# An attention loop laid out anew: other places for the transposes, the mask and the turned values

## The reference

```python
def _dequant_matmul(x, qw, scales):
    w = (qw.astype(jnp.float32) - ZERO) * jnp.repeat(scales, GS, axis=0)
    return x @ w
q = _dequant_matmul(hidden_states, qw_q, scales_q)   # 32 heads of 128
k = _dequant_matmul(hidden_states, qw_k, scales_k)   # 8 heads
v = _dequant_matmul(hidden_states, qw_v, scales_v)   # 8 heads
...
q, k = _apply_rope(q, cos, sin), _apply_rope(k, cos, sin)
k, v = jnp.repeat(k, rep, axis=1), jnp.repeat(v, rep, axis=1)
scores = jnp.einsum('bhqd,bhkd->bhqk', q, k) / math.sqrt(HD)
scores = jnp.where(causal[None, None], scores, jnp.finfo(scores.dtype).min)
attn = jax.nn.softmax(scores.astype(jnp.float32), axis=-1)
ctx = jnp.einsum('bhqk,bhkd->bhqd', attn, v)
return _dequant_matmul(ctx, qw_o, scales_o)
```

## Time and profile before

| | us |
|---|---|
| median of three executions | 559.31 |
| lowest, highest | 554.47, 561.33 |
| the profiled execution: its own time | 560.78 |
| its span on the core | 558.7 |
| PE busy | 534.9 (96%) |
| DVE, ACT, POOL busy | 477.6, 429.0, 383.3 |

### The profile page before, as it was taken

One profiled execution on the slowest core, in us unless ns is written; L12 is line 12 of the kernel. 1 busy time (PEld: TensorE's weight loads), 2 busy tenths in 40 slices (PEclk: granted clock), 3 DMA queues, 4 the chain that ended last, 5 costly groups with the idle time before them and its releaser, 6 DMA issues.

```text
span 558.7 us, 10860 instructions
## 1 busy us (share of the span) xinstructions
PE 534.9 (96%) x3190; PEld 332.7 (60%) x3190; DVE 477.6 (85%) x629; ACT 429.0 (77%) x1091; POOL 383.3 (69%) x400
## 2 busy tenths in 40 slices
PE   8999979999999999999999999999999999987985
PEld 6744456666666666666666666666666666653442
DVE  4885957999899899989998999899989998876897
ACT  3574558878888888788878887888788878876795
POOL 3005485799779877987799779867986897741063
PEclk9989999999999999999999999999999999999899
DMA  8931344742673267327733672367336532410003
GB/s 295 271 74 38 82 107 133 170 95 57 170 178 88 57 177 175 79 66 177 176 69 75 176 181 61 82 177 168 70 82 169 131 79 72 96 38 1 1 20 132
DMA packets 41341, 63.47 MB, mean 114 GB/s; under 512 B 12452, under 2 KB 20804, under 8 KB 41316
## 3 DMA queue, kind: packets, MB, share of 16 engines
q1 hardware_dynamic: 35652, 46.94, 32.3%
q0 software_dynamic: 3648, 12.75, 11.3%
q10 hardware_dynamic: 2016, 3.48, 2.0%
HBM read 28.55 MB, written 2.10 MB: 55 GB/s over the span
## 4 chain that ended last, share of the span: by engine, by line
PE 82%; DVE 8%; ACT 4%; issue 2%; DMA 2%; POOL 1%; ACTq 0%; SPq 0%; DVEq 0%; POOLq 0%
PE pair L1578 22%; PE pair L1579 22%; PE flow L1702 11%; PE flow L1567 9%; PE flow L1694 6%; PE pair L1485 3%; PE pair L1507 1%; DVE y_max L1361 1%; DMA swap_q<-raw_q 1%; PE flow L1572 1%; DVE accT L1265 1%; ACT probs L779 1%; PE flow L1485 1%; DVE probs L1373 1%; DVE rope_c L1373 1%
## 5 line engine op out<-in xcount | busy, mean ns | idle before, releaser
L1265 DVE SCALAR_TENSOR_TENSOR accT<-pair,so_now,accT 128x1024 f32<-128x1024 f32 x103 | 130.9, 1277 | 19.8 <-PE pair L1579 16.2
L1249 DVE SCALAR_TENSOR_TENSOR raw_q<-pair,sc_now,raw_q 128x1024 f32<-128x1024 f32 x90 | 115.4, 1282 | 7.0 <-ACT raw_q L835 3.9
L572 POOL TENSOR_TENSOR rope_s<-swap_q,consts 128x512 f32<-128x512 f32 x62 | 85.4, 1378 | 30.6 <-DMA swap_q<-raw_q 30.6
L1578 PE MATMUL pair<-ctx_hi,wo 128*128 128x512 f16 x256 | 97.0, 379 | 4.2 <-issue 2.3
L1579 PE MATMUL pair<-ctx_lo,wo 128*128 128x512 f16 x256 | 97.0, 379 | 0.0
L1578 PE MATMUL pair<-h_hi,wq 128*128 128x512 f16 x240 | 91.0, 379 | 0.2 <-ACT raw_q L835 0.2
L779 ACT ACTIVATE probs<-flow,negmax 128x128 f32<-128x128 f32 x248 | 87.3, 368 | 4.9 <-DVE negmax L1217 4.9
L1579 PE MATMUL pair<-h_lo,wq 128*128 128x512 f16 x240 | 91.0, 379 | 0.0
L584 POOL TENSOR_TENSOR qT<-rope_c,rope_s 128x512 f32<-128x512 f32 x62 | 85.5, 1379 | 4.6
L572 POOL TENSOR_TENSOR rope_c<-raw_q,consts 128x512 f32<-128x512 f32 x62 | 77.6, 1274 | 10.7 <-DVE raw_q L1249 10.3
L1702 PEld LDWEIGHTS flow<-probsT,v_now 128*128 128x128 f32 x512 | 62.9, 193 | 19.2 <-ACT probsT L841 15.3
(11 more groups left out here) (281 smaller groups left out, 1008.5 us busy)
## 6 DMA issues: line engine op xcount, KB each, us to landing
swap_q<-raw_q SPq DMA_DIRECT2D x62, 256.0 KB, 3.7
accT<-part_out POOLq DMA_DIRECT2D x22, 512.0 KB, 4.5
wq_i<-in_L_attn_qw_q SPq DMA_DIRECT2D x8, 1024.0 KB, 5.6
wo_i<-in_L_attn_qw_o SPq DMA_DIRECT2D x32, 256.0 KB, 2.8
swap_k<-raw_k SPq DMA_DIRECT2D x14, 256.0 KB, 3.6
wkv_i<-in_L_attn_qw_k SPq DMA_DIRECT2D x8, 256.0 KB, 3.7
wkv_i<-in_L_attn_qw_v SPq DMA_DIRECT2D x8, 256.0 KB, 4.1
stage<-in_x ACTq DMA_DIRECT2D x4, 256.0 KB, 4.7
```

The source lines that it names most:

```text
L572: pool.tensor_tensor(per_seq(into[:, f, :]), per_seq(source[:, f, :]), on_each_seq(table), ALU.mult).then_inc(done, 1)
L1249: dve.scalar_tensor_tensor(out=into, in0=flat(pair[pair_of(h, (kind, j), last, first)][:, :, :]), scalar=sc_now[:, scale_slot(kind, h), j: ...
L1265: dve.scalar_tensor_tensor(out=a, in0=flat(pair[pair_of(h, (O, c), last, first)][:, :, :]), scalar=so_now[:, (h if c == 0 else h - 1) % 2, ...
L1578: pe.matmul(into[:, f, :], w, upper[:, half[f]], start=True, stop=False)
```

## The change

All lists of the loop are written anew.

- TensorE: `turn_probs(0)` stands one step earlier (behind `(Q, 1)`), with two steps between it and `context(0)`; `turn_probs(1)` no longer follows `context(0)` directly but one step later, and `(O, 2)` stands between it and `context(1)`. Heads 2 and 3 of the last group keep their order.
- The mask: ScalarE writes it in head 3 as well (`SEEDED` is gone). The matmul that added it goes, in all groups but the last.
- The values: one step `(VALUES, 0)` of eight transposes into `pair[2]` in head 3, copied by ScalarE as one 128x1024 instruction in place of two of 128x512.
- ScalarE: the exponentials of half 0 come first in a head; `dequant` of the weights moves from the head's start to its end (`output_weights`, `dequant_q`) or between (`dequant_kv`); `part_output` comes after the output weights.
- VectorE: `inverse(1)` comes behind the drain of `(Q, 1)`; `inverse(0)` of the next head is taken at the end of a head, between the drain of `(O, 0)` and `maxima(1)`; `(O, 2)` is added before `split_context(1)`.
- POOL: in head 0 `normalise(0)` comes before the sine product. SP: `load_q` and `load_kv` before the swaps of head 1, `load_output` behind them.

```diff
@@ the steps
-                  [(Q, 0), (O, 1), (Q, 1), (Q, 2), (Q, 3), (V, 0), (V, 1), (O, 2), (O, 3), (V, 2), (O, 0)],
-                  [(Q, 0), (O, 1), (Q, 1), (Q, 2), (V, 3), (Q, 3), (O, 2), (O, 3), (O, 0)]]
+                  [(Q, 0), (O, 1), (Q, 1), (Q, 2), (Q, 3), (V, 0), (O, 2), (V, 1), (O, 3), (V, 2), (O, 0)],
+                  [(Q, 0), (O, 1), (Q, 1), (Q, 2), (V, 3), (Q, 3), (O, 2), (VALUES, 0), (O, 3), (O, 0)]]
...
-            return at % 3 if at < len(STEPS) - 1 else 1
+            return at % 3 if at < len(STEPS) - 1 else 2
...
-        SEEDED = REP - 1
-
         def seeded(h, last):
 
-            return h < SEEDED and not (last and h >= 2)
+            return not (last and h >= 2)
@@ POOL
-                    if first and h == 0:
+                    if h == 0:
                         normalise(0)
                     if ahead:
                         q_sine(0)
-                    if not (first and h == 0):
+                    if h > 0:
                         normalise(0)
@@ ScalarE
-                    def keep_values(turned, f):
-
-                        act.wait_ge(vT_done, 2 * turned + f + 1)
-                        act.activation(v_now[:, HB * f:HB * f + HB, :], per_seq(flow[f][:, :]), ACT.Copy).then_inc(v_kept, 1)
+                    def keep_values():
+
+                        act.wait_ge(step_done, steps_by(g, h, (VALUES, 0), first, last))
+                        act.activation(v_flat, flat(pair[pair_of(h, (VALUES, 0))][:, :, :]), ACT.Copy).then_inc(act_drained, 1)
...
                     if not (first and h == 0):
                         exps(n, 0, score_bank(0, last and h == 3))
-                        if present(h, (Q, 0), first, last):
-                            drain_query()
+                    if h < 2 and not last and not (first and h == 0):
+                        dequant_kv(g + 1, h)
+                    if present(h, (Q, 0), first, last):
+                        drain_query()
                     exps(n, 1, score_bank(1, last and h == 3))
...
+                    seed_mask(0)
                     keep_upper_context(1)
+                    output_weights()
                     if h == 3 and not last:
-                        keep_values(g + 1, 0)
-                    if not (first and h == 0):
-                        seed_mask(0)
+                        keep_values()
+                    part_output()
                     seed_mask(1)
-                    part_output()
+                    if h < REP - 1 and present(h + 1, (Q, 0), False, last) or h == REP - 1 and not last:
+                        dequant_q(g + (h + 3) // REP, (h + 3) % REP)
@@ VectorE
-                    inverse(0)
+                    if first and h == 0:
+                        inverse(n, 0)
                     add_output(1)
-                    if not (first and h == 0):
-                        inverse(1)
...
                         drain(*((V, 3) if h == 3 and j == 3 else (Q, j)))
-                        if first and h == 0 and j == 1:
-                            inverse(1)
+                        if j == 1 and not (last and h >= 2):
+                            inverse(n, 1)
...
                     add_output(0)
+                    if not (last and h == 3):
+                        inverse(n + 1, 0)
                     if not (last and h >= 2):
                         maxima(n + 1, 1)
@@ TensorE
-                            turn_values(f, flow[f])
+                    def values_ahead():
+
+                        pe.wait_ge(dve_drained, drains_by(g, h, (V, 3), first, last))
+                        free_pair(VALUES, 0)
...
+                    project(Q, 1)
+                    if not (first and h == 0):
+                        turn_probs(0)
+                    project(Q, 2)
+                    if first and h == 0:
+                        turn_probs(0)
+                    project(*((V, 3) if h == 3 else (Q, 3)))
+                    context(0)
+                    project(*((K, 0), (K, 2), (V, 0), (Q, 3))[h])
+                    turn_probs(1)
+                    output(2)
                     if h == 2:
-                        project(V, 0)
                         project(V, 1)
+                    context(1)
                     if h == 3:
-                        project(Q, 3)
-                    context(1)
...
+                        values_ahead()
+                    output(3)
                     scores_ahead(0)
```

More of the change, by code:

```diff
@@ L264, in present @@
                 return False
-            return not (last and (s[0] in (K, V) or s[0] == Q and h >= 2))
+            return not (last and (s[0] in (K, V, VALUES) or s[0] == Q and h >= 2))
         def added_by_dma(h, s, last):
@@ L480, in body @@
                     n = REP * g + h
-                    if h < 2 or not last:
-                        load_output(g + h // 2, (h + 2) % REP)
                     if h == 1 and not last:
                         load_q(g + 1)
+                        if loads:
+                            load_kv(g + 2)
                     if present(h, (Q, 3), first, last):
@@ L494, in body @@
                         swap(swap_k, raw_k, swapped_k)
+                    if h < 2 or not last:
+                        load_output(g + h // 2, (h + 2) % REP)
             body(0, True, False)
@@ L1288, in body @@
                         drain(K, 2)
+                    if h == 3:
+                        drain(Q, 3)
+                    if not (last and h >= 2):
+                        add_output(2)
                     if h == 2:
                         drain(V, 1)
-                    if h == 3:
-                        drain(Q, 3)
                     split_context(1)
                     if not (last and h >= 2):
-                        add_output(2)
                         add_output(3)
@@ L1697, in context @@
                     def context(f):
-                        if h == 0:
-                            pe.wait_ge(v_kept, 2 * g + f + 1)
+                        if first and h == 0:
+                            pe.wait_ge(v_kept, f + 1)
+                        elif h == 0:
+                            pe.wait_ge(act_drained, drains_by(g, -1, (VALUES, 0), first, last))
                         pe.wait_ge(probsT_kept, 2 * n + f + 1)
@@ L1704, in context @@
                         mm.then_inc(pv_done, 1)
-                    def values_ahead(f):
-                        if h == 3 and not last:
-                            if f == 0:
-                                pe.wait_ge(dve_drained, drains_by(g, h, (V, 3), first, last))
-                            pe.wait_ge(ctx_split, 2 * n + f + 1)
-                            turn_values(f, flow[f])
+                    def values_ahead():
+                        pe.wait_ge(dve_drained, drains_by(g, h, (V, 3), first, last))
+                        free_pair(VALUES, 0)
+                        into = pair[pair_of(h, (VALUES, 0))]
+                        for f in range(2):
+                            for b in range(HB):
+                                mm = pe.transpose(into[:, f, seq(b)], raw_v[:, f, seq(b)], ident)
+                        mm.then_inc(step_done, 1)
                     def scores_ahead(f):
@@ L1729, in body @@
                     output(1)
-                    project(Q, 1)
-                    project(Q, 2)
-                    if not last:
-                        turn_probs(0)
-                    project(*((V, 3) if h == 3 else (Q, 3)))
                     if last and h >= 2:
@@ L1737, in body @@
                         output(3)
-                    if last:
                         turn_probs(0)
```

73 lines of the change are left out of this document (24 added, 49 removed).

## The result

The changed kernel takes 543.02 us (median of four executions, 541.43 to 544.40). The kernel before, in the same session, takes 558.54 us. The ratio is 0.9736, with a 95% interval of 0.9691 to 0.9780, so the change is faster by 2.6%. The forecast was 546 us, range 543 to 555. The profiled execution took 544.21 us, with a span of 542.4 us.

A forecast was written before the change was run, and what follows sets the result against it. TensorE, without idle time in the loop, was taken to bound the kernel. Savings of 11.0 (groups 1 to 6), 1.5 (group 0), 1.1 (first head) and 0.3 us (last group) make 13.9, giving 546 us, range 543 to 555.

The forecast's parts named there:

- The slots: On TensorE, context of half 0 and transposes of half 1 together save 0.32 us a head, 1.28 a group.
- The masks: Two mask matmuls of 0.28 us, pause included, leave TensorE in each of groups 0 to 6: 0.56 a group.
- Costs at nothing: ScalarE's mask in head 3, the values' single step, and the new VectorE and POOL orders would cost nothing.
- transposes 0: Tightest joint in a head: POOL's normalising done at 2.2 to 2.3 us, transposes of half 0 due at 2.59.
- The swap and the loads: SP's earlier loads let head 1's query swap meet less traffic; cost nothing, bounds 0 to 2 us in all.
- First head: Its context of half 0 waited 1.97 us for ScalarE; 1.1 us saved, bounds 0 and 2.0.
- last group: Its transposes of half 1 wait 0.32 us for ScalarE; 0.15 saved in heads 0 and 1, 0.3 together.
- Second, joints late: One joint of each head late by 0.25 us, some 30 heads lose 7.5: 554 us; chance 0.18.
- Third, masks alone: Contexts of half 0 keep 1.15 us, only the mask matmuls' 3.9 us is gained: 556.9 us; chance 0.10.
- Fourth, VectorE waits for the exponentials: VectorE's reciprocal of half 0 waits 1.4 us a head for ScalarE's late exponentials, 27 us lost: 573 us; chance 0.05.

The follow-up runs named there:

- e3: Changed kernel with the transposes of half 1 right behind the context of half 0 again: 551.50 us, ratio 0.9891 to the kernel before.
- e4: Changed kernel with the transposes of half 0 one step later again, leaving one step before the context of half 0: 547.04 us, ratio 0.9835 to the kernel before.
- e10: Changed kernel with one extra, unread ScalarE copy of 512 columns per head in groups 0 to 6, ahead of the exponentials of half 0: 543.65 us.
- e1: Changed kernel with the mask of head 3 added by a TensorE matmul again, values still one step into a pair: 546.76 us.
- e6: Changed kernel with POOL's sine product of head 0 ahead of its normalising again: 545.81 us, ratio 0.9796 to the kernel before.
- e7: Kernel before with only TensorE's transposes of half 1 one step later and (O, 2) before the context of half 1: 563.89 us, ratio 1.0108.
- e9: Changed kernel with a second step, (O, 3), between transposes and context of half 1 in heads 0 and 1: 550.23 us.
- e11: Kernel before with the same TensorE move as e7, and ScalarE's mask of half 0 ahead of the upper context of half 1: 561.00 us, ratio 1.0062.
- e5: Changed kernel with VectorE's reciprocal of half 0 at the next head's start again, behind the maxima of half 1: 550.32 us.
- e12: Changed kernel with key and value loads behind head 1's query swap again, and ScalarE's mask of half 1 ahead of its part output: 543.66 us.
- c0: The changed kernel run again without edits: 544.61 us, ratio 0.9765 to the kernel before.
- e8: Changed kernel with SP's key and value loads behind head 1's query swap again, as in the kernel before: 542.69 us.

## Why the prediction was right

**The slots.** Right as predicted: context 0 at 0.89, transposes 1 at 0.43 in every head of the loop, context 1 at 0.98 in three heads of four, a group of 53.43 against 53.4. The slots of both kernels give the 1.28 a group directly: four times 1.15 - 0.89 and 0.49 - 0.43. e3 shows the cause that I had read from the earlier trace rows. That it also costs 1.27 is in part chance: its contexts lose 0.30 to 0.41 each, not 0.26, and contexts of half 1 give 0.27 back.

By the Trainium skill (TensorE: Matmul & The Clock Gate, Step-by-step) weight loads are pulled ahead of the matmuls in flight. The traces agree with this where the input is there: with a step more the load stands 0.21 ahead (211.38 against 211.59), and with one step less (e4) it starts with the matmuls and the slot grows by 0.09. Where a load waits up to 0.28 us and other matmuls still run, as in e10, nothing is lost.

**The masks.** The 0.56 a group came out, but I named one cause for two: the matmul is 0.43 of it, and the 0.13 of pauses goes with the values' way through a pair (e1).

**Costs at nothing.** The mask by ScalarE in head 3, the values' step, POOL and VectorE's list cost nothing, as said. Where I had ScalarE's exponentials of half 0 against VectorE I got a margin of 0.4; e10 measures 0.43 for heads 2 and 3 and 0.26 for head 1. In what I expected of e10 I left this margin out and took only that of transposes 0, so that 0.3 was to come through, and TensorE lost nothing. Mistakes in what I expected of the experiments have the same root, in both directions: e6 and e10 were to cost more, since I let each delay run through to TensorE; e7, e9 and e11 were to be faster than they are, since I looked at the joint that I moved and not at the next.

**The swap and the loads.** "It meets less traffic than before" was wrong as an argument. The swap still lands in 3.7, but the loads, now issued earlier, meet the part output's transfer, which I had not looked at: 8.5 us instead of 5.7 at most, and 0.34 to 0.98 us lost once in an execution. It lies within the 0 to 2 us that I allowed.

**First head and last group.** The first head gave 1.26 for 1.1: its context waits 0.54 less, but still waits. With a scatter of up to 0.9 between executions the closeness of these two numbers is luck.

```profile
78.53 1.13 PE L1703 MATMUL flow<-probsT,v_now 128*128 128x128 f32 x8 [1.43 <-ACT probsT L839]
```

Before it was 1.97. The last group gave 1.21 for 0.3. Of this 0.55 is in heads 0 and 1, at the upper bound of my term. The other 0.66 is a pause of TensorE between its heads 2 and 3 in the trace before, at 497.43, that is gone; I had costed nothing there because these heads keep their order on TensorE, and this term of the sum was too small by that path. The path runs over other engines: TensorE's next output step needs VectorE's lower contexts, which stand behind an add that waits for POOL's transfer of the part output, and POOL issues that transfer behind its normalising of half 0, so behind VectorE's reciprocal. VectorE's wait for the transfer is 2.87 us before and 2.21 in the changed kernel. e5, with the reciprocal late again, has 2.87 and a pause of 0.73 again (0.81 before, 0.15 in the changed kernel). So most of it was the early reciprocal.

**The rivals.** *Second, joints late:* no joint of the loop was late but by the transfer, and once by POOL's normalising (0.06, the group of 53.49); e5 and e9 show what it would have been (1.06 and 0.84 a group). *Third, masks alone:* falls with e3; the placing of the transposes is worth 1.28 a group, the mask matmuls 0.43. *Fourth, VectorE waits for the exponentials:* e10 shows how it would begin (with 0.52 us of delay the reciprocal is 0.09 to 0.26 late) and that TensorE does not pay for it yet; no run has the delay of 1.41 with which I priced it. Of the 3 us between forecast and median, 0.9 is the last group, and 0.8 is the kernel before, whose median is 558.54 with a fourth execution and was 559.31 with three; the rest is less than the four executions of the changed kernel lie apart (541.43 to 544.40).

## What to carry to other kernels

Where the bounding engine shows no idle time, compare the slots of the same instruction at different places: a slot that is longer than the shortest holds the wait of its own load or of the next instruction, and one step of other work between two dependent pieces takes it out. Moving a piece on that engine moves what the others get: before the move, write down for each engine the work that now arrives later and what is queued behind it there, one joint further than the one moved (e7, e9 and e11 failed at the next joint, by 0.25 to 0.64 us at a time). A delay of another engine costs only what exceeds its room, so measure the room with a useless instruction (e10) before taking it as a bound.

## What was not expected of the hardware

- Waits of 0.21 to 0.28 us on a weight load cost its matmuls nothing (e10), one of 0.37 cost 0.09 (e12), one of 0.61 cost 0.34 (e5: last step matmul at 211.29, so due at 211.51, begun at 211.79, record 0.66).
- A transfer that adds 512 KB to a sum in SBUF took 4.4 to 5.8 us, and 8.5 and 9.1 with 1 MB of weight loads issued 2.9 us ahead of it and 0.5 MB in the last 0.9 us (changed kernel and c0; in e8, without the 0.5 MB, 5.8 at most). In other groups the same issues did not delay it as much.
- The same first context started between 78.00 and 79.84 us: a difference of two profiled spans below 1.8 us says nothing of a change here, while the loop groups of each of these kernels, without a late transfer, agree within 0.07.
